# Full attention: three score banks, four item banks, steps written out, a new order of a step

## What is computed

```
scores = einsum('bhqd,bhkd->bhqk', qh, kh) / sqrt(16)      # 512 queries x 1601 keys
scores = where(mask == 0, -1e9, scores)
attn   = softmax(scores, axis=-1)
context = einsum('bhqk,bhkd->bhqd', attn, vh)
```

## Time and profile before

| what | us |
|---|---|
| median of three runs | 5217.95 |
| lowest, highest | 5210.15, 5223.06 |
| span of the profiled execution | 5209.4 |
| full attention in it: first score to last value block | 1556.5 to 3950.2 |
| DVE busy, ACT busy (union over the span) | 3852.0, 2767.8 |

### The profile page before, as it was taken

One profiled execution on the slowest core, in us unless ns is written; L12 is line 12 of the kernel. 1 busy time (PEld: TensorE's weight loads), 2 busy tenths in 40 slices (PEclk: granted clock), 3 DMA queues, 4 the chain that ended last, 5 costly groups with the idle time before them and its releaser, 6 DMA issues. The chain is left out here.

```text
span 5209.4 us, 96256 instructions
## 1 busy us (share of the span) xinstructions
PE 4733.7 (91%) x28783; PEld 2782.8 (53%) x28784; DVE 3852.0 (74%) x7481; ACT 2767.8 (53%) x5099; POOL 1289.2 (25%) x996
## 2 busy tenths in 40 slices
PE   8979997999579999999999999999997803999999
PEld 4546664777244444444444444444444602888887
DVE  7766665664758888887888888888894723877886
ACT  2225552222327777877777777777783101444443
POOL 5630001221631101110110110111001264554544
PEclk9989998999779999999999999999997756999999
DMA  7766663220872332443334334333314654333332
GB/s 216 222 183 166 161 167 114 82 83 33 269 167 48 67 77 58 76 78 70 56 65 80 61 71 78 74 52 72 60 35 111 182 174 122 61 63 81 59 62 37
DMA packets 326842, 519.92 MB, mean 100 GB/s; under 512 B 50000, under 2 KB 242863, under 8 KB 324192
## 3 DMA queue, kind: packets, MB, share of 16 engines
q1 hardware_dynamic: 294816, 461.48, 36.4%
q0 software_dynamic: 28208, 51.82, 4.7%
q10 hardware_dynamic: 3360, 0.98, 0.1%
HBM read 254.97 MB, written 179.55 MB: 83 GB/s over the span
## 5 line engine op out<-in xcount | busy, mean ns | idle before, releaser
L1185 DVE TENSOR_REDUCE full_peak<-full_item 128x1 f32<-128x512 f32 (+2 forms) x3392 | 2025.7, 654 | 339.9 <-PE full_item L1247 323.9
L1161 ACT ACTIVATE full_prob<-full_score 128x512 f32<-128x512 f32 (+1 forms) x3328 | 1744.9, 601 | 401.3 <-PE full_score L1257 386.1
L1247 PE MATMUL full_item<-full_kst,full_qst 49*128 49x512 f32 (+1 forms) x4096 | 1171.0, 403 | 8.5 <-DMA full_kst<-full_high 5.2
L1257 PE MATMUL full_score<-full_qst,full_kst 51*128 51x512 f32 (+1 forms) x3328 | 1028.8, 434 | 8.7 <-issue 7.6
L1247 PEld LDWEIGHTS full_item<-full_kst,full_qst 49*128 49x128 f32 x4096 | 618.8, 188 | 603.6 <-DVE full_peak L1185 538.6
L1267 PE MATMUL full_value<-full_prob,full_vaug 128*17 128x512 f32 x6656 | 879.2, 600 | 0.6 <-ACT full_prob L1161 0.4
L1257 PEld LDWEIGHTS full_score<-full_qst,full_kst 51*128 51x128 f32 (+1 forms) x3328 | 504.9, 182 | 371.7 <-ACT full_prob L1161 294.4
L1100 POOL TENSOR_TENSOR full_low<-full_low,full_keep 128x1601 f32<-128x1601 f32 x32 | 116.0, 3625 | 2020.0 <-ACT full_low L1135 2020.0
L2550 ACT ACTIVATE moe_h<-moe_hbank,moe_b 128x512 f32<-128x512 f32 (+1 forms) x320 | 200.0, 625 | 450.5 <-PE moe_hbank L2643 445.4
L2653 PE MATMUL moe_ybank<-moe_w_both,moe_h_high 128*128 128x512 f32 x1088 | 386.6, 399 | 0.1
L754 DVE TENSOR_REDUCE win_peak<-win_item 128x2 f32<-128x384 f32 x512 | 262.2, 552 | 124.1 <-PE win_item L794 117.1
(11 more groups left out here) (274 smaller groups left out, 7278.9 us busy)
## 6 DMA issues: line engine op xcount, KB each, us to landing
full_kst<-full_high SPq DMA_DIRECT2D x256, 200.1 KB
full_ctxT<-in_ctxT SPq DMA_DIRECT2D x16, 1601.0 KB, 9.2
full_kst<-full_low SPq DMA_DIRECT2D x128, 200.1 KB
win_qst<-scratch_q SPq DMA_DIRECT2D x384, 64.0 KB, 2.7
full_qst<-scratch_q SPq DMA_DIRECT2D x384, 64.0 KB
scratch_xbuf<-ctxp_zero POOLq DMA_DIRECT2D x17, 1032.0 KB, 7.7
moe_x<-scratch_xbuf SPq DMA_DIRECT2D x32, 516.0 KB, 3.8
scratch_attn<-win_raw SPq DMA_DIRECT2D x64, 256.0 KB, 2.1
```

What stands on the lines that cost most here:

```text
L1161: nc.scalar.activation(prob_of(s, h, kt)[0:rows, :], score[score_bank(u)][0:rows, :], ACT.Exp, scale=SCALE).then_inc(score_read, 1)
L1185: nc.vector.tensor_reduce(peak[s.par][:, hq:hq + len(qts), c], src, AX, ALU.max).then_inc(item_read, 1)
L1247: ins = nc.tensor.matmul(ps[:, at:at + z - a], qst[s.slot][rows, h // 2, qt * P:(qt + 1) * P].bitcast(F32R), kst[s.slot][rows, h // 2, a:z ...
L1257: nc.tensor.matmul(score[score_bank(u)][0:z - a, :], kst[s.slot][rows, h // 2, a:z].bitcast(F32R), qst[s.slot][rows, h // 2, :].bitcast(F3 ...
```

## The change

The score banks go from four to three and the item banks from three to four; `STEP_ORDER` and `ITEM_HALVES` are new, with the same 52 S, 54 I, 13 V and 4 J. The 64 steps are written out, without a loop, so bank numbers need not repeat with the loop's body.

```diff
@@ -517,13 +517,8 @@
 def windows_by_batch(eng, body):
 
 
-    for k in range(8):
-        body(Step(0, k), k == 0, 2)
-    with eng.Fori(1, BATCH // 4) as j:
-        for k in range(16):
-            body(Step(j * 4 - 2, k), False, 2)
-    for left in (7, 6, 5, 4, 3, 2, 1, 0):
-        body(Step(0, STEPS - 1 - left), False, min(left, 2))
+    for k in range(STEPS):
+        body(Step(0, k), k == 0, min(STEPS - 1 - k, 2))
 
 
 class Eighth:
@@ -852,7 +847,7 @@
     HQ = GROUP * QT
     LINKS = 2
     VW = HD + 1
-    SCORE_BANKS = 4
+    SCORE_BANKS, ITEM_BANKS = 3, 4
     PROB_BUFS = 4
 
     SCORES = [(h, kt) for kt in range(KT) for h in range(GROUP)]
@@ -867,9 +862,9 @@
     KEY_JOBS = [[("K", c, j) for j in range(4)] for c in range(KC)]
     VALUE_JOBS = [("V", tiles, None) for tiles in VTILES]
     JOBS = [KEY_JOBS[0], VALUE_JOBS[0:4], KEY_JOBS[1], VALUE_JOBS[4:8]]
-    STEP_ORDER = ("SSISIVISSIISJSIISISJISISSIVISISSISVSSIIIJIISSISVSISISISVIISSISVSIISSSIIIVISIISVISSIIVSISISIVISSISIJI"
-                  "SISSISIVISISSIVSIISSIVI")
-    ITEM_HALVES = ("010101010101101010110111001111101111110110111101010111")
+    STEP_ORDER = ("ISISSIVSISISIISSSISIIJSISIIIJISSIVSISISIVISSIISVSISIISVSISIISVSIISSIVISSIJISIISSISIVSSJSISIVISIISSIV"
+                  "SISIISVSISIISVSISIISVSI")
+    ITEM_HALVES = "011010110110101010101010101010101001010100111010101010"
     READ_VALUES_AT = 8
     ALL_JOBS = [j for part in (0, 2, 1, 3) for j in JOBS[part]]
     EXPS = KT * GROUP
@@ -930,19 +925,17 @@
         if left >= 2:
             items += [("max", s.plus(2), j) for j in range(AHEAD, HEAD)]
         base = len(prologue) + PER_WINDOW * s.n
-        at = len(prologue) + PER_WINDOW * (s.k % 3)
-        return [(*it, base + n, (at + n) % 3) for n, it in enumerate(items)]
+        return [(*it, base + n, (base + n) % ITEM_BANKS) for n, it in enumerate(items)]
 
     def turn_number(s):
 
-        if isinstance(s.n, int) and s.n == 0:
+        if s.n == 0:
             return NMAX
         return len(prologue) + PER_WINDOW * (s.n - 1) + (NMAX - HEAD) + (AHEAD if not (isinstance(s.n, int) and s.n == STEPS - 1) else 0)
 
     prologue = ([("max", Step(0, 0), j) for j in range(NMAX)] + [("turn", Step(0, 0), 0)]
                 + [("max", Step(0, 1), j) for j in range(HEAD)])
-    prologue = [(*it, n, n % 3) for n, it in enumerate(prologue)]
-    assert PER_WINDOW % 3 == 0
+    prologue = [(*it, n, n % ITEM_BANKS) for n, it in enumerate(prologue)]
 
     def place(h, qt):
 
@@ -952,17 +945,15 @@
 
         return s.turn % 2 if isinstance(s.turn, int) else s.k // 4 % 2
 
-    def score_bank(u):
-
-        return (len(ALL_JOBS) + u) % SCORE_BANKS
-
-    assert UNITS % SCORE_BANKS == 0 and EXPS % SCORE_BANKS == 0
+    def score_bank(s, u):
+
+        return (first_unit(s) + u) % SCORE_BANKS
 
     with ExitStack() as ctx:
         sp_ = Space(nc, ctx, "full")
         sb, ps = sp_.sb, sp_.ps
         score = [ps(f"score{i}", [P, 512]) for i in range(SCORE_BANKS)]
-        item_bank = [ps(f"item{i}", [P, 512]) for i in range(3)]
+        item_bank = [ps(f"item{i}", [P, 512]) for i in range(ITEM_BANKS)]
         value = ps("value", [P, SQ])
 
         kst = [sb(f"kst{i}", [STACK, 2, SK]) for i in range(4)]
@@ -1152,13 +1143,13 @@
                 base = first_unit(s)
                 for u, (kind, e) in enumerate(units(s)):
                     if kind == "job":
-                        read_job(base + u, score_bank(u), JOBS[s.slot][e], s.turn + 1, 1 - batch_par(s))
+                        read_job(base + u, score_bank(s, u), JOBS[s.slot][e], s.turn + 1, 1 - batch_par(s))
                         continue
                     h, kt = SCORES[e]
                     rows = min(P, SK - kt * P)
                     act.wait_ge(score_full, base + u + 1)
                     at_least(act, value_done, KT * s.n + kt - PROB_BUFS + 1)
-                    nc.scalar.activation(prob_of(s, h, kt)[0:rows, :], score[score_bank(u)][0:rows, :], ACT.Exp,
+                    nc.scalar.activation(prob_of(s, h, kt)[0:rows, :], score[score_bank(s, u)][0:rows, :], ACT.Exp,
                                          scale=SCALE).then_inc(score_read, 1)
                     if e == READ_VALUES_AT and not first:
                         read_values(s.plus(-1))
@@ -1231,7 +1222,7 @@
                     ins.then_inc(score_full, 1)
 
             def item(kind, s, j, number, bank):
-                at_least(pe, item_read, number - 2)
+                at_least(pe, item_read, number - ITEM_BANKS + 1)
                 ps = item_bank[bank]
                 if kind == "turn":
                     pe.wait_ge(parts_done, s.n + 1)
@@ -1254,7 +1245,7 @@
                 at_least(pe, score_read, first_unit(s) + u - SCORE_BANKS + 1)
                 a, z = kt * P, min(kt * P + P, SK)
                 rows = slice(64 * (h % 2), 64 * (h % 2) + ROWS)
-                nc.tensor.matmul(score[score_bank(u)][0:z - a, :], kst[s.slot][rows, h // 2, a:z].bitcast(F32R),
+                nc.tensor.matmul(score[score_bank(s, u)][0:z - a, :], kst[s.slot][rows, h // 2, a:z].bitcast(F32R),
                                  qst[s.slot][rows, h // 2, :].bitcast(F32R), start=True, stop=True).then_inc(score_full, 1)
 
             def values(s, kt):
@@ -1284,7 +1275,7 @@
                         scores(s, u, *SCORES[units(s)[u][1]])
                         u += 1
                     elif token == "J" and busy(s):
-                        job(first_unit(s) + u, score_bank(u), JOBS[s.slot][units(s)[u][1]], s.turn + 1, 1 - batch_par(s))
+                        job(first_unit(s) + u, score_bank(s, u), JOBS[s.slot][units(s)[u][1]], s.turn + 1, 1 - batch_par(s))
                         u += 1
                     elif token == "I":
                         for it in items[given:given + 1]:
```

## The result

| | us | ratio to before, 95% interval |
|---|---|---|
| before, median | 5218.82 (5210.15 to 5223.06, four runs) | |
| changed kernel, median | 5309.8 (5302.71 to 5320.63, four runs) | 1.0174, 1.0156 to 1.0191 |
| span of the profiled execution | 5300.9 | |

What follows compares the result with a forecast made beforehand. The prediction took the order itself, its blocks and turns, to bound the stage. It summed -19.4 (loop) + 37 (order and score banks, net) - 3 (item banks) to +15 us, 5233 us, with an eight-in-ten range of 5190 to 5280.

Steps and rivals of the forecast that it cites:

- The order as the bound: Stage with jobs: blocks and the turns of the order's string bound it; the old order runs almost without bank waits.
- stretches: Runs of scores and items between the value blocks and jobs, 17 a step; 18.2 us a step in the old order.
- The loop: Two returns of the loop, removed by writing out the steps: 19.4 us saved, 10 as the low end.
- Fewer turns: New order in steps: turns are paired starts on different array halves; stretches 17.0 us against 18.2, 1.2 us a step on offer.
- three score banks: Scores wait for ACT's read of the one three before: +2.07 us in slots 0 and 2, about 1.55 in 1 and 3.
- The stretch of seven: Seven scores and seven items before the first job: 3.31 us against 2.25, +1.05, as ACT sets the pace.
- 4+4: Stretch of four scores and four items, 1.40 us without waits; the fourth score waits from 0.81 to 1.26: +0.23.
- 4+5: Stretch of four scores, five items, 1.40 us without waits: +0.40 after a key job, +0.3 after a value job or one tile.
- the short job with the 2+2 behind it: Fourth job in slots 0 and 2: the two scores before it are still being read, +0.39.
- 3+4 with the turn matmul: Stretch of three scores, four items and a matmul needing the whole array (0.25 us counted, 0.1 to 0.5): 1.15 us.
- Four item banks: Fourth item bank: worth nothing in steps with jobs; a longer lead for DVE saves 3 us in the last steps (0 to 6).
- The clock: Rival: the clock drops in the long stretch, 7 us each, 60 times, some +400 us; chance 0.02.

Runs made afterwards that it cites:

- the short-stretch one: The changed kernel (three score, four item banks, steps written out) with another order and other halves, its largest stretch 5 scores and 6 items: 5183.8 us, 0.9943 of before.

## Why the prediction was wrong

- **The order as the bound: right.** The old order ran without waits, as its 18.2 us of stretches said (written out, PE is busy 149.04 of 149.04 us), and both halves of the change taken alone behaved as the walk through them gave (161.9 and 160.1 us a batch for 161).
- **The loop: right.** 19.4 us in the steps concerned, and 0.2 us a batch besides; the written-out kernel with the old order came out 15.7 us faster than the runs of before beside it, and in the profiled execution 13 us were given back in the last steps.
- **Fewer turns, three score banks: right in sum and in part.** Undisturbed steps of slots 0 to 3 have 19.0, 18.5, 19.0 and 18.5 us of stretches, where the working had 19.07 and 18.55 in turn. The stretch of seven took the 3.31 us of the working, 4+4 1.56 in place of 1.63, 4+5 1.84 for 1.80, the short job with the 2+2 behind it 1.68 for 1.68, 3+4 with the turn matmul 1.15 for 1.15. A batch cost 2.3 us more, for 2.5 forecast.
- **Four item banks: right in steps with jobs** (nothing), not for the last steps, which were to gain 3 us and lost 9.7, at a clock of 0.89 in place of 0.97.
- **The clock: the step that failed.** It stood among the rivals with a chance of 0.02 and some 400 us. It was put at nothing in the sum. The mechanism is real and its place was named, and it costs 65 us in the 60 steps with jobs. I dismissed it on the two jobless steps of the earlier trace rows, at a clock of 1.00 although PE waits for DVE there. But those waits, 1.8 us in two steps, are spread over them in gaps of at most 0.55 us. The fault was to take the sum of idle time for what counts. And the price was taken from the loop's return, after 3.5 to 4 us without any matmul, as if it came in each step; it comes in two steps of five and mostly for 3.4 us. With 65 us for it the sum gives 15 + 65 = 80, and 12.7 us more for the last steps come to 93, against 91 measured. Why it comes in some steps and not in others stays open.
- **The rule that I cited was the better guide.** The Trainium skill, "TensorE: Matmul & The Clock Gate", section "A second HAM failure mode: psum-queue depth-cycling", says that brief idle times of PE between groups, while it cycles through PSUM banks, make the clock swing between its two levels. The 25 dips to 0.50 here, and their absence once the waiting scores are doubled, agree with it in what they do to the clock, though PE's row shows no idle time in that stretch, only one half of the array at work; the old order with three score banks, with more idle time and 4 dips, shows that it does not hold for every such wait.
- **Two slips of no weight.** The chance of a faster kernel adds up to 0.19 (0.08 and half of 0.22), not 0.20; and the four steps between the marks of the earlier trace rows are steps 17 to 20, still in the loop's first pass.

## What to carry to other kernels

Walk the written order by a few measured durations (pair, block, round trip of a bank, pace of the reader): it gave each stretch of the changed kernel within 0.1 us. Then ask a second question of the longest run of waits: where PE trickles at its reader's pace for 3.3 us, the clock cost as much again as the waiting (about 1.05 us a step each, 65 us in 60 steps), while waits of 0.3 to 0.5 us spread over the step cost little but themselves. When the bank count changes, the order has to be made anew for it, and a stretch should not ask for many more results of one reader than it has banks: in these kernels seven on three banks brought dips, five on three banks none. To test for the clock, double the matmuls that wait, and see whether the kernel gets faster.

## What the runs showed of the hardware that I had not expected

- Adding 256 needless matmuls made a kernel 50 us faster (5309.8 to 5259.3); the granted clock of its steps with jobs is 1.00 instead of 0.97.
- The granted clock fell to 0.50 where PE's row has hardly any idle time ahead of it (4.26 of 4.42 us busy before the dip at 1954.02). What sets the place apart is that matmuls come one at a time there, on half of the array, for about 1 us. In the old order with three score banks PE idles more, 3.6 us a batch, and there are 4 dips.
- The dips come in a pattern, not in every step that has the cause: 25 in 60 steps that are alike, in slots 0 and 2 mostly, of 3.4, 6.8 or 10.2 us.
- The clock of the last four steps is 0.97, 0.89, 0.86 and 0.86 in the kernel before, the changed one, the written-out and the short-stretch one, for nearly the same work. The order of those steps is the same in the first and the third.
